# Macaron transformer block on one core: the light layers' token sum on VectorE stands ahead of its wait for the probabilities of the same pass

## The chip, the cores and the metric

One core of a Trainium2 chip runs the whole kernel as one launch. The metric is device time in microseconds (us), the median of several executions. One further execution was taken by the hardware profiler; all rows below are from it. Engines: TensorE (PE in the rows; PEld is its weight load), VectorE (DVE), ScalarE (ACT), GpSimd (POOL), SyncE (SP, the DMA queue).

## The reference, cut to what matters

8192 tokens (16 sequences of 512) of 128 channels go through six layers. Layers one and three are the same routed feed-forward layer with the same weights; each has a light part (attention in windows of 128 tokens, 8 heads of 64) and a heavy part on chosen tokens. What concerns the change is the light part and the sum onto the tokens:

```python
def light_local_attn(x, gamma, wq, wkv, wo):
    xn = rmsnorm(x, gamma)
    q = xn @ wq
    k, v = jnp.split(xn @ wkv, 2, axis=-1)
    # windows of 128 tokens, 8 heads
    attn = jax.nn.softmax(einsum('bwhid,bwhjd->bwhij', q * SCALE, k), axis=-1)
    out = einsum('bwhij,bwhjd->bwhid', attn, v)
    return out @ wo
...
x = x + 0.5 * _L0_ffn_ref(_layernorm(x), ...)   # layer 1 (f1)
x = x + _L0_attn_ref(_layernorm(x), ...)
x = x + 0.5 * _L0_ffn_ref(_layernorm(x), ...)   # layer 3 (f2)
```

Beside it the layer's router runs 50 iterations of a coordinate descent on 48 rows of 512 scores (`coor_descent`: a log-sum-exp, then a clamp), and then picks the top tokens.

## The kernel before, in words

`light_attention` runs twice, with tag `f1l` in layer one and `f2l` in layer three. There are 64 windows (`NT`), and they are software-pipelined: `windows` calls `body(i, ...)` on every engine for i = -1 to 66, and pass i works on several windows at once. Most passes are hardware loops unrolled by four (`Fori`), where addresses and semaphore values come out of registers; a few passes at the seams are written out. Each engine runs its own part of the pass strictly in the order written, and semaphores tie the engines together.

A pass on each engine, by line:

- TensorE: L400 the q and k projections of window i (`ps_qk`); L407 the output projection of window i-3 into `ps_a[:, 2]` (signals `f_ps`); L415 eight transposes of the probabilities of window i-2; L420 the v projection; L425 the transpose of the next window's normed tokens `xr` into `ps_a[:, 0]`, the same PSUM bank as L407's result, so that it waits for `y_ready`, the token sum of this same pass; L433 the scores of window i (`ps_s`); L449 probabilities times v (`ps_v`), which waits for ScalarE's copies of the turned probabilities and of v.
- ScalarE: L474 copies the attention output to `oT` (L407 of this pass reads it), L479 the exponential into `prob` (signals `p_sb`), L484 copies q and k, L465 and L467 exponential and logarithm of one descent step, L490 turned probabilities, L493 v, L496 the turned tokens `xrT`, then the second descent step.
- VectorE: L534 maximum of the scores, L538 subtracts it (`ssub`), L528, L522 and L523 settle one descent step and start the next (`na`, `nm`, `tmin`), L546 sums the probabilities (`rsum`, waits for `p_sb`), L550 reciprocal (`rec`), L554 the token sum `y = x + 0.5 * ps_a[:, 2]` (waits for `f_ps`; `g_y` in layer one, `g_x` in layer three), L513 makes `xr` of the window after next (it waits for L425, which reads the buffer before), then L528, L522 and L523 again for the second descent step.
- GpSimd: L371, two multiplications of half of the probabilities by `rec`, right after `rec_ready`.

The passes fall into stages. In passes 4 to 27 (24 passes, a hardware loop) the descent runs, two steps to a pass, and VectorE makes `xr`. In passes 28 to 59 ScalarE makes `xr` (L460) and VectorE instead picks eight maxima to a pass (L570, L573); of these, 32 to 59 (28 passes) are hardware loops.

Of the kernel before, what the change touches and what calls it, by code (L numbers as in the profile page):

```python
# [12 lines left out]
ALU = mybir.AluOpType  # L13
# [50 lines left out]
def past(i, n):  # L64

    return not isinstance(i, int) or i >= n
# [192 lines left out]
def light_attention(nc, tag, x, y, scale_a, shift_b, s_rows, smax, na, logk, posw, wparts, lw, hw, w, ident):  # L259
# [7 lines left out]
    with ExitStack() as ctx:  # L267
# [35 lines left out]
        ps_a = A.ps("ps_a", [P, 4, P])  # L303
# [3 lines left out]
        sum_ready, rec_ready, norm_ready, y_ready = (A.sem(n) for n in ("sum_ready", "rec_ready", "norm_ready", "y_ready"))  # L307
        xrT_ps, qk_ps, v_ps, s_ps, pT_ps, o_ps, f_ps = (
            A.sem(n) for n in ("xrT_ps", "qk_ps", "v_ps", "s_ps", "pT_ps", "o_ps", "f_ps"))
# [13 lines left out]
        def windows(eng, body, between):  # L323


            for i in range(-1, VB):
                body(i, i % VB, 0 if i == D0 else None, None)
            with eng.Fori(1, D1 // VB) as k:
                for u in range(VB):
                    body(VB * k + u, u, 2 * (VB * k) + 2 * (u - D0) - 1, None)  # L330
            for i in range(D1, D1 + VB):
                body(i, i % VB, None, i - D1)
            with eng.Fori(D1 // VB + 1, (D1 + RQ) // VB) as k:
                for u in range(VB):
                    body(VB * k + u, u, None, VB * k + u - D1)
            between(1)
            with eng.Fori((D1 + RQ) // VB, E0 // VB) as k:
                for u in range(VB):
                    body(VB * k + u, u, None, VB * k + u - D1)
            between(2)  # L340
            for i in range(E0, NT + 3):
                body(i, i % VB, None, None)

        def live(i, lag=0):
            return not isinstance(i, int) or 0 <= i - lag < NT

        def late(i, r):
            return r is not None or isinstance(i, int) and i >= D1

        def at(i, n):  # L350
            return isinstance(i, int) and i == n

        @block.sync
        def _(sp):
            sp.dma_start(hraw[:, 0:HID], w["wq_heavy"]).then_inc(hw_in, 16)
            sp.dma_start(hraw[:, HID:3 * HID], w["wkvT_heavy"]).then_inc(hw_in, 16)
            sp.dma_start(hgamma[:], w["gamma_heavy"].rearrange("(c o) -> c o", o=1)).then_inc(hw_in, 16)
            sp.dma_start(hw["wo"][:], w["wo_heavy"].rearrange("(p r) c -> r p c", r=P)).then_inc(hw_in, 16)
            sp.wait_ge(hw_in, 64)
# [148 lines left out]
        @block.vector  # L508
        def _(dve):
            ch = Chain(dve, step)  # L510

            def make_xr(j):
                nc.vector.scalar_tensor_tensor(xr[:], x[:, bass.ds(j, 1), :].rearrange("p o c -> p (o c)"), scale_a[:, bass.ds(j, 1)],  # L513
                                               shift_b[:, bass.ds(j, 1)].broadcast_to([P, C]), ALU.mult, ALU.add).then_inc(xr_ready, 1)

            make_xr(0)

            def descend(d):
                if past(d, 1):
                    dve.wait_ge(na_ready, d)  # L520
                    nc.vector.nop(nofuse=True)
                nc.vector.tensor_scalar(nm[:], smax[:], na[:], -1.0, ALU.min, ALU.mult)  # L522
                nc.vector.tensor_scalar(tmin[:], s_rows[:], na[:], None, ALU.min).then_inc(tmin_ready, 1)  # L523

            def settle(d):
                dve.wait_ge(lsum_ready, d + 1)
                nc.vector.nop(nofuse=True)
                nc.vector.tensor_scalar(na[:], lsum[:], nm[:], logk[:], ALU.subtract, ALU.subtract).then_inc(na_ready, 1)  # L528

            def body(i, u, d, r):  # L530
                if live(i, 1):
                    dve.wait_ge(s_ps, i)
                    sc = ps_s[:].rearrange("p s a b -> p (s a) b")
                    nc.vector.tensor_reduce(mx[:], sc, X_AX, ALU.max).then_inc(mx_ready, 1)  # L534
                    dve.wait_ge(mx_ready, i)
                    if past(i, 2):
                        dve.wait_ge(p_sb, i - 1)
                    nc.vector.tensor_tensor(ssub[:], sc, mx[:].rearrange("p (h o) -> p h o", o=1).broadcast_to([P, HEADS, P]),  # L538
                                            ALU.subtract).then_inc(sub_ready, 1)
                if d is not None:  # L540
                    if past(d, 1):
                        settle(d - 1)
                    descend(d)
                if live(i, 1):
                    dve.wait_ge(p_sb, i)
                    nc.vector.tensor_reduce(rsum[:], prob[(u - 1) % 2][:], X_AX, ALU.add).then_inc(sum_ready, 1)  # L546
                    dve.wait_ge(sum_ready, i)
                    if past(i, 3):
                        dve.wait_ge(norm_ready, 2 * i - 4)
                    nc.vector.reciprocal(rec[(u - 1) % 2][:], rsum[:]).then_inc(rec_ready, 1)  # L550
                if live(i, 3):
                    dve.wait_ge(f_ps, i - 2)
                    j = i - 3
                    nc.vector.scalar_tensor_tensor(  # L554
                        y[:, bass.ds(j, 1), :].rearrange("p o c -> p (o c)"), ps_a[:, 2], 0.5,
                        x[:, bass.ds(j, 1), :].rearrange("p o c -> p (o c)"), ALU.mult, ALU.add).then_inc(y_ready, 1)
                if live(i, -2) and not late(i, r):
                    dve.wait_ge(xrT_ps, i + 2)
                    make_xr(i + 2)
                if d is not None and past(d, 1):  # L560
                    settle(d)
                    descend(d + 1)
                if at(i, D1):
                    settle(ITERS - 2)
                    dve.wait_ge(na_ready, ITERS - 1)
                    nc.vector.tensor_scalar(tmin[:], s_rows[:], na[:], 0.0, ALU.subtract, ALU.min).then_inc(u_ready, 1)
                if r is not None:
                    dve.wait_ge(work_ready, r + 1)
                    nc.vector.nop(nofuse=True)
                    nc.vector.max(top[:], work[:]).then_inc(top_ready, 1)  # L570
                    dve.wait_ge(top_ready, r + 1)
                    nc.vector.nop(nofuse=True)
                    nc.vector.match_replace(work[:], top[:], work[:], -1.0).then_inc(work_ready, 1)  # L573
                if at(i, E0):
                    dve.wait_ge(filled, 1)
                    ch.step(nc.vector.tensor_tensor_scan(rank[:], ones[:], mask[:], 0.0, ALU.mult, ALU.add))
                if at(i, E0 + 1):
                    ch.step(nc.vector.tensor_tensor(rank[:], rank[:], mask[:], ALU.mult))
                    nc.vector.tensor_scalar(rank[:], rank[:], -1.0, None, ALU.add).then_inc(rank_ready, 1)
                if at(i, NT + 1):  # L580
                    dve.wait_ge(rows_ps, 1)
                    ch.step(nc.vector.tensor_copy(posw[:], ps_rows))
                    ch.step(nc.vector.tensor_copy(wparts[:, 0], posw[:, 1]))
                    ch.step(nc.vector.tensor_tensor(wrest[:], posw[:, 1], wparts[:, 0], ALU.subtract))
                    ch.step(nc.vector.tensor_copy(wparts[:, 1], wrest[:]))
                    ch.step(nc.vector.tensor_tensor(wparts[:, 2], wrest[:], wparts[:, 1], ALU.subtract))

            def between(n):
                if n == 1:
                    dve.wait_ge(work_ready, RQ + 1)  # L590
                    ch.step(nc.vector.tensor_scalar(mask[0:KV0, :], work[0:KV0, :], -1.0, None, ALU.is_equal))
                if n == 2:
                    dve.wait_ge(work_ready, RKV + 1)
                    ch.step(nc.vector.tensor_scalar(mask[KV0:ROWS, :], work[KV0:ROWS, :], -1.0, None, ALU.is_equal))

            windows(dve, body, between)


# [1826 lines left out]
```

## Time and profile before

| | |
|---|---|
| median of 3 executions | 3347.32 us (3339.31 to 3350.53) |
| the profiled execution | 3347.39 us |
| its span | 3345.6 us |
| granted TensorE clock, mean | 0.902 |
| TensorE busy | 2784.1 us (83%) |
| VectorE busy | 2343.1 us (70%) |
| ScalarE busy | 1850.5 us (55%) |
| GpSimd busy | 1479.8 us (44%) |

The span is the time between the first and the last instruction; the execution's own time has 1.8 us around it. The light part of layer one lies between about 54 and 534 us of the span, that of layer three between about 1592 and 2099 us.

### The profile page before, as it was taken

The numbers are of one execution on the slowest core, as the hardware profiler recorded it, in microseconds if no ns is written. First come the engines' busy times: TensorE is split into PE (matmuls) and PEld (weight loads), VectorE is DVE, ScalarE is ACT, GpSimd is POOL, SyncE is SP. The second block draws the span as 40 slices with busy tenths as digits, with TensorE's granted clock in tenths as the row PEclk, the third lists the DMA queues.
The fourth block names the chain that finished last, engine by engine and source line by source line (L and its number), as shares of the span: only waits on it lengthen the run. The fifth ranks groups of instructions, "written<-read, shape, count | busy, mean of one in ns | idle before, by whom it ended". The sixth has DMA issues, their size and how long they took to land. (4 is left out here: it accounts for less than half of the span.)

```text
span 3345.6 us, 72967 instructions
## 1 busy us (share of the span) xinstructions
PE 2784.1 (83%) x24552; PEld 1858.4 (56%) x24552; DVE 2343.1 (70%) x6126; ACT 1850.5 (55%) x3771; POOL 1479.8 (44%) x1662
## 2 busy tenths in 40 slices
PE   7999998996699999998888999899584278887674
PEld 4777886785233333333666777687452045555542
DVE  5887776885589888983777777688752267776741
ACT  3776664552167666664677666455431257775421
POOL 1222336772455555531222233776445254541445
PEclk9999999997599999999999999899785579999775
DMA  2000000001333333320000000000432355453532
GB/s 79 0 0 1 0 0 1 0 0 30 76 85 88 79 78 78 87 49 13 14 0 0 1 0 1 1 0 0 120 95 36 88 130 131 123 128 81 135 88 31
DMA packets 157597, 162.91 MB, mean 49 GB/s; under 512 B 43217, under 2 KB 136017, under 8 KB 157009
## 3 DMA queue, kind: packets, MB, share of 16 engines
q1 hardware_dynamic: 148176, 152.43, 17.6%
q0 software_dynamic: 9216, 7.87, 1.7%
q8 instruction: 114, 1.87, 0.2%
q14 instruction: 91, 0.74, 0.1%
HBM read 84.57 MB, written 74.60 MB: 48 GB/s over the span
## 5 line engine op out<-in xcount | busy, mean ns | idle before, releaser
L1700 DVE CUSTOM_DVE_ANT_0 la_ps<-la_ps,la_tri 128x512 f32<-128x512 f32 (+3 forms) x1024 | 481.0, 516 | 89.9 <-PE la_ps L1281 80.8
L1554 ACT ACTIVATE la_prob<-la_ps 128x512 f32<-128x512 f32 x640 | 373.8, 601 | 231.2 <-PE la_ps L1292 224.4
L371 POOL TENSOR_TENSOR f2l_prob<-f2l_prob,f2l_rec 128x512 f32<-128x512 f32 x128 | 132.4, 1056 | 361.2 <-DVE f2l_rec L550 361.2
L1281 PE MATMUL la_ps<-la_ks,la_qs 48*128 48x512 bf16 (+3 forms) x1024 | 255.1, 318 | 42.5 <-DVE la_mx L1700 26.8
L1181 POOL TENSOR_SCALAR_AFFINE_SELECT la_prob<-la_prob 128x512 f32<-128x512 f32 x256 | 160.0, 637 | 293.5 <-ACT la_prob L1554 293.3
L371 POOL TENSOR_TENSOR f1l_prob<-f1l_prob,f1l_rec 128x512 f32<-128x512 f32 x128 | 133.9, 1068 | 332.5 <-DVE f1l_rec L550 332.5
L1292 PE MATMUL la_ps<-la_qs,la_ks 50*128 50x512 bf16 (+3 forms) x1024 | 240.9, 308 | 5.1 <-ACT la_prob L1554 2.3
L1698 DVE TENSOR_REDUCE ca_mx<-ca_ps 128x4 f32<-128x512 f32 x256 | 162.7, 681 | 51.3 <-PE ca_ps L1281 51.1
L1324 PE MATMUL la_ps_o<-la_prob,la_v 128*32 128x512 f32 (+3 forms) x2048 | 195.7, 456 | 0.0
L1292 PEld LDWEIGHTS la_ps<-la_qs,la_ks 50*128 50x128 bf16 x1024 | 67.1, 94 | 231.2 <-ACT la_prob L1554 168.9
L1554 ACT ACTIVATE ca_prob<-ca_ps 128x512 f32<-128x512 f32 x256 | 140.3, 598 | 40.8 <-PE ca_ps L1292 38.9
L1700 DVE DVE_READ_ACCUMULATOR2_ANT la_mx<- 128x1 f32 x1024 | 144.8, 141 | 0.0
L400 PE MATMUL f2l_ps_qk<-f2l_xrT,f_wqkv 128*128 128x128 f32 x1024 | 133.0, 284 | 0.7 <-ACT f2l_xrT L496 0.7
L400 PE MATMUL f1l_ps_qk<-f1l_xrT,f_wqkv 128*128 128x128 f32 x1024 | 132.6, 283 | 0.7 <-ACT f1l_xrT L496 0.7
L1292 PE MATMUL ca_ps<-ca_qs,ca_ks 58*128 58x128 bf16 x1024 | 93.0, 226 | 45.1 <-DMA ca_ks<-stack_image 18.9
L1281 PEld LDWEIGHTS la_ps<-la_ks,la_qs 48*128 48x128 bf16 x1024 | 66.9, 95 | 111.7 <-DVE la_mx L1700 92.4
L400 PEld LDWEIGHTS f2l_ps_qk<-f2l_xrT,f_wqkv 128*128 128x128 f32 x1024 | 120.7, 194 | 11.7 <-issue 10.5
L400 PEld LDWEIGHTS f1l_ps_qk<-f1l_xrT,f_wqkv 128*128 128x128 f32 x1024 | 120.5, 193 | 11.7 <-issue 10.5
L1292 PEld LDWEIGHTS ca_ps<-ca_qs,ca_ks 58*128 58x128 bf16 x1024 | 62.0, 98 | 107.8 <-issue 65.6
L1166 POOL TENSOR_TENSOR ca_rr<-ca_qb,ca_t 128x512 f32<-128x512 f32 x32 | 43.7, 1366 | 169.2 <-ACT ca_t L1623 169.2
L546 DVE TENSOR_REDUCE f2l_rsum<-f2l_prob 128x8 f32<-128x1024 f32 x64 | 78.1, 1220 | 55.8 <-ACT f2l_prob L479 55.8
L546 DVE TENSOR_REDUCE f1l_rsum<-f1l_prob 128x8 f32<-128x1024 f32 x64 | 78.1, 1220 | 54.5 <-ACT f1l_prob L479 54.5
(552 smaller groups left out, 7990.5 us busy)
## 6 DMA issues: line engine op xcount, KB each, us to landing
stack_image<-la_parts SPq DMA_DIRECT2D x192, 128.0 KB, 2.4
stack_image<-ca_parts SPq DMA_DIRECT2D x192, 128.0 KB, 2.3
la_qs<-stack_image SPq DMA_DIRECT2D x64, 192.0 KB, 3.5
la_ks<-stack_image SPq DMA_DIRECT2D x64, 192.0 KB, 4.3
ca_qs<-stack_image SPq DMA_DIRECT2D x64, 192.0 KB, 3.9
ca_ks<-stack_image SPq DMA_DIRECT2D x64, 192.0 KB, 5.1
gather_table<-m_xn SPq DMA_DIRECT2D x32, 256.0 KB, 2.3
gather_table<-m_pr SPq DMA_DIRECT2D x32, 128.0 KB, 2.2
```

What stands on the lines that cost most here:

```text
L371: nc.gpsimd.tensor_tensor(pr[:, g], pr[:, g], rc[:, g].rearrange("p (h o) -> p h o", o=1).broadcast_to([P, PAIRS, P]), ALU.mult).then_inc( ...
L400: last = nc.tensor.matmul(ps_qk[:, t, p], wqkv[:, t, p * P:(p + 1) * P], xrT[:], start=True, stop=True)
L546: nc.vector.tensor_reduce(rsum[:], prob[(u - 1) % 2][:], X_AX, ALU.add).then_inc(sum_ready, 1)
L1166: nc.gpsimd.tensor_tensor(rr[:], left[:], right[:], op)
L1181: return nc.gpsimd.affine_select(view, view, pattern=[[0, 4], [1, P]], compare_op=ALU.is_ge, fill=0.0, base=0, channel_multiplier=-1)
L1281: last = nc.tensor.matmul(bank[:, col:col + width], qs[u][rows, h // 2, qblk * P:(qblk + 1) * P], ks[u][rows, h // 2, keys], start=True, s ...
L1292: last = nc.tensor.matmul(bank[:, col:col + width], ks[u][rows, h // 2, blk * P:(blk + 1) * P], qs[u][rows, h // 2, blk * P:blk * P + widt ...
L1324: last = nc.tensor.matmul(ps_o[32 * j:32 * j + 32, blk * P:T], v[u][:, blk, 4 * q + j, :], prob[q % 2][:, unit, col:col + width], start=bl ...
L1554: nc.scalar.activation(prob[q % 2][:, n], ps2[n % 2][:], ACT.Exp, scale=SM).then_inc(S["p_sb"], 1)
L1698: last = nc.vector.tensor_reduce(m, bank[:].rearrange("p (a b) -> p a b", a=TPB), X_AX, ALU.max)
L1700: last = nc.vector.tensor_tensor_reduce(bank[:, col:col + width], bank[:, col:col + width], tri[:, T - width:T], 1.0, -BIG, ALU.add, ALU.m ...
```

## The change

On VectorE the token sum (its wait for `f_ps` and the instruction) moves from behind the reciprocal to ahead of the wait for `p_sb`, in every pass that has one, in both light layers. No other engine's code is touched, and no wait is added or dropped.

```diff
                     descend(d)
+                if live(i, 3):
+                    dve.wait_ge(f_ps, i - 2)
+                    j = i - 3
+                    nc.vector.scalar_tensor_tensor(
+                        y[:, bass.ds(j, 1), :]..., ps_a[:, 2], 0.5,
+                        x[:, bass.ds(j, 1), :]..., ALU.mult, ALU.add).then_inc(y_ready, 1)
                 if live(i, 1):
                     dve.wait_ge(p_sb, i)
                     nc.vector.tensor_reduce(rsum[:], prob[(u - 1) % 2][:], X_AX, ALU.add).then_inc(sum_ready, 1)
...
                     nc.vector.reciprocal(rec[(u - 1) % 2][:], rsum[:]).then_inc(rec_ready, 1)
-                if live(i, 3):
-                    dve.wait_ge(f_ps, i - 2)
-                    j = i - 3
-                    nc.vector.scalar_tensor_tensor(
-                        y[:, bass.ds(j, 1), :]..., ps_a[:, 2], 0.5,
-                        x[:, bass.ds(j, 1), :]..., ALU.mult, ALU.add).then_inc(y_ready, 1)
                 if live(i, -2) and not late(i, r):
                     dve.wait_ge(xrT_ps, i + 2)
                     make_xr(i + 2)
```

Lines after it shift: in the changed kernel the token sum is L547, the sum of probabilities L552 and the reciprocal L556. On VectorE, a pass of layer three in the descent stage stood like this before, from the end of the first descent step to the making of `xr` (ISA and REGISTER_ALU rows are register instructions that the engine's sequencer does, for addresses and semaphore values):

```order
L523 TENSOR_SCALAR f2l_tmin<-f_s_rows,f_na 48x512
L545 ISA
L546 TENSOR_REDUCE f2l_rsum<-f2l_prob 128x8
L547 ISA
L549 ISA
L550 RECIPROCAL f2l_rec<-f2l_rsum 128x8
L552 ISA
L554 ISA x2
L554 SCALAR_TENSOR_TENSOR g_x<-f2l_ps_a,g_y 128x128
L558 ISA
L513 ISA x2
L513 REGISTER_ALU
```

And it stands like this in the changed kernel:

```order
L523 TENSOR_SCALAR f2l_tmin<-f_s_rows,f_na 48x512
L545 ISA
L547 ISA x2
L547 SCALAR_TENSOR_TENSOR g_x<-f2l_ps_a,g_y 128x128
L551 ISA
L552 TENSOR_REDUCE f2l_rsum<-f2l_prob 128x8
L553 ISA
L555 ISA
L556 RECIPROCAL f2l_rec<-f2l_rsum 128x8
L558 ISA
L513 ISA x2
L513 REGISTER_ALU
```

The token sum and its register instructions moved ahead of the sum of the probabilities; `xr` now follows the reciprocal directly. In layer one there are fewer register instructions; the same place of the descent stage, changed kernel:

```order
L523 TENSOR_SCALAR f1l_tmin<-f_s_rows,f_na 48x512
L547 ISA
L547 SCALAR_TENSOR_TENSOR g_y<-f1l_ps_a,g_x 128x128
L552 TENSOR_REDUCE f1l_rsum<-f1l_prob 128x8
L555 ISA
L556 RECIPROCAL f1l_rec<-f1l_rsum 128x8
L558 REGISTER_ALU
L513 ISA
L513 SCALAR_TENSOR_TENSOR f1l_xr<-g_x,g_a,g_b 128x128
```

One register instruction stands ahead of the token sum here and two in layer three; ahead of `xr` it is one here (the ISA row of L513) and three there. On the other engines the order of instructions is the same in both kernels.

## Rows read from the trace of the kernel before

**Rows 1.** Busy time by stretch, L479 alone (length, ACT busy, its count)

```profile
90.70:258.60 167.90, 23.27 (x22) 1.00 0.00 0
302.60:488.50 185.90, 27.48 (x26) 1.00 0.00 0
1629.90:1816.30 186.40, 23.31 (x22) 1.00 0.00 0
1861.30:2053.50 192.20, 27.48 (x26) 1.00 0.00 0
```

**Rows 2.** Waits in the first, third and fourth stretch (total us, times, longest)

```profile
PE f1l_ps_a L425 <- DVE g_y L554: 11.2, 22, 0.6
...
PE f2l_ps_a L425 <- DVE g_x L554: 25.1, 22, 1.2
...
PE f2l_ps_a L425 <- DVE g_x L554: 8.9, 26, 1.0
```

**Rows 3.** Timeline, one pass of layer one's descent stage (start, us, engine, line, idle before)

```profile
197.61 1.06 ACT L479 ACTIVATE f1l_prob<-f1l_ssub 128x1024 f32<-128x1024 f32 x1 [0.95 <-DVE f1l_ssub L538]
198.70 1.22 DVE L546 TENSOR_REDUCE f1l_rsum<-f1l_prob 128x8 f32<-128x1024 f32 x1 [0.33 <-ACT f1l_prob L479]
...
200.22 0.29 DVE L554 SCALAR_TENSOR_TENSOR g_y<-f1l_ps_a,g_x 128x128 f32 x1
200.34 2.09 POOL L371 TENSOR_TENSOR f1l_prob<-f1l_prob,f1l_rec 128x512 f32<-128x512 f32 x2 [5.51 <-DVE f1l_rec L550]
...
200.66 0.30 PE L425 MATMUL f1l_ps_a<-g_ident,f1l_xr 128*128 128x128 f32 x1 [0.46 <-DVE g_y L554]
201.14 0.38 DVE L513 SCALAR_TENSOR_TENSOR f1l_xr<-g_x,g_a,g_b 128x128 f32 x1 [0.63 <-PE f1l_ps_a L425]
201.36 0.59 ACT L493 COPY f1l_v<-f1l_ps_v 128x512 f32<-128x512 f32 x1
201.94 0.76 DVE L523 TENSOR_SCALAR f1l_tmin<-f_s_rows,f_na 48x512 f32<-48x512 f32 x1
...
205.01 1.06 PE L407 MATMUL f1l_ps_a<-f_wo,f1l_oT 128*128 128x128 f32 x8
205.29 1.06 ACT L479 ACTIVATE f1l_prob<-f1l_ssub 128x1024 f32<-128x1024 f32 x1 [0.74 <-DVE f1l_ssub L538]
```

**Rows 4.** Timeline, one pass of layer three's descent stage

```profile
1697.76 1.06 ACT L479 ACTIVATE f2l_prob<-f2l_ssub 128x1024 f32<-128x1024 f32 x1 [0.99 <-DVE f2l_ssub L538]
...
1700.53 2.04 POOL L371 TENSOR_TENSOR f2l_prob<-f2l_prob,f2l_rec 128x512 f32<-128x512 f32 x2 [6.43 <-DVE f2l_rec L550]
1700.98 0.33 PE L425 MATMUL f2l_ps_a<-g_ident,f2l_xr 128*128 128x128 f32 x1 [1.20 <-DVE g_x L554]
1701.80 0.92 DVE L513 SCALAR_TENSOR_TENSOR f2l_xr<-g_y,g_a,g_b 128x128 f32 x1 [0.87 <-PE f2l_ps_a L425]
...
1705.37 1.15 PE L407 MATMUL f2l_ps_a<-f_wo,f2l_oT 128*128 128x128 f32 x8
1706.24 1.06 ACT L479 ACTIVATE f2l_prob<-f2l_ssub 128x1024 f32<-128x1024 f32 x1 [1.00 <-DVE f2l_ssub L538]
```

**Rows 5.** Timeline, layer one's late stage, a pass where TensorE does not wait

```profile
431.85 1.06 PE L407 MATMUL f1l_ps_a<-f_wo,f1l_oT 128*128 128x128 f32 x8
434.69 0.30 PE L425 MATMUL f1l_ps_a<-g_ident,f1l_xr 128*128 128x128 f32 x1
438.92 1.06 PE L407 MATMUL f1l_ps_a<-f_wo,f1l_oT 128*128 128x128 f32 x8
```

**Rows 6.** Timeline, one pass of layer three's late stage

```profile
1987.35 1.06 PE L407 MATMUL f2l_ps_a<-f_wo,f2l_oT 128*128 128x128 f32 x8
1988.36 1.22 DVE L546 TENSOR_REDUCE f2l_rsum<-f2l_prob 128x8 f32<-128x1024 f32 x1 [1.24 <-ACT f2l_prob L479]
1990.17 0.59 ACT L493 COPY f2l_v<-f2l_ps_v 128x512 f32<-128x512 f32 x1
1994.64 1.06 ACT L479 ACTIVATE f2l_prob<-f2l_ssub 128x1024 f32<-128x1024 f32 x1 [1.04 <-DVE f2l_ssub L538]
```

More of the change, by code:

```diff
@@ L543, in body @@
                     descend(d)
+                if live(i, 3):
+                    dve.wait_ge(f_ps, i - 2)
+                    j = i - 3
+                    nc.vector.scalar_tensor_tensor(
+                        y[:, bass.ds(j, 1), :].rearrange("p o c -> p (o c)"), ps_a[:, 2], 0.5,
+                        x[:, bass.ds(j, 1), :].rearrange("p o c -> p (o c)"), ALU.mult, ALU.add).then_inc(y_ready, 1)
                 if live(i, 1):
@@ L550, in body @@
                     nc.vector.reciprocal(rec[(u - 1) % 2][:], rsum[:]).then_inc(rec_ready, 1)
-                if live(i, 3):
-                    dve.wait_ge(f_ps, i - 2)
-                    j = i - 3
-                    nc.vector.scalar_tensor_tensor(
-                        y[:, bass.ds(j, 1), :].rearrange("p o c -> p (o c)"), ps_a[:, 2], 0.5,
-                        x[:, bass.ds(j, 1), :].rearrange("p o c -> p (o c)"), ALU.mult, ALU.add).then_inc(y_ready, 1)
                 if live(i, -2) and not late(i, r):
```

## Prediction, made before the changed kernel was timed

> **What bounds the kernel now.** I read first how long a pass takes. The exponential (L479) runs once a pass, so the length of a stretch over its count is the pass time [rows 1]: 167.90 / 22 = 7.63 us in layer one's descent stage, 185.90 / 26 = 7.15 in its late stage, 186.40 / 22 = 8.47 and 192.20 / 26 = 7.39 in the same stages of layer three. The second column of times there says nothing more, but the clock (the 1.00 behind the count) does: TensorE ran at its full level throughout, so no stage is slow for that.
>
> Then I read who waits for the token sum. TensorE's L425 does, in every pass: 11.2 us over 22 passes of layer one's descent stage (0.51 a pass), 25.1 over 22 in layer three (1.14), 8.9 over 26 in its late stage (0.34) [rows 2]. All of that wait goes away in the best case. Whether a pass gets shorter by it is the question, so I followed one pass in each timeline.
>
> Layer one, descent [rows 3]. Exponential at 197.61, sum of probabilities at 198.70 (1.09 later), GpSimd's pair at 200.34 (1.64 later) until 202.43, the end of `tmin` at 201.94 + 0.76 = 202.70, which is 0.27 behind GpSimd's end, and the next exponential at 205.29 (2.59 later). 1.09 + 1.64 + 2.09 + 0.27 + 2.59 = 7.68, the whole pass. The reader is to see that the token sum (200.22) and L425 are not in this chain: `tmin` is held until GpSimd has finished both halves. `xr` starts at 201.14, 0.18 behind the end of L425, and ends at 201.52, 0.13 behind the middle of the pair (200.34 + 1.04 = 201.38): it is held too, but by the first half alone.
>
> The Trainium skill (SBUF — State Buffer, section Who interferes with whom) says that VectorE shares a port pair with GpSimd, taken for a whole instruction by whoever starts first, and that VectorE wants it for two SBUF inputs while GpSimd reads SBUF (`xr`), and in the fast modes of `tensor_scalar` (`tmin`). The trace agrees with it. It is the rule that speaks against the change: without it, in the sum for layer three's descent stage below, `xr` would end at 3.66 + 0.38 = 4.04 and `tmin` at 4.04 + 0.42 + 0.76 = 5.22 at the latest instead of 5.72, which would make 0.25 a pass or 6 us more of gain.
>
> Layer three, descent [rows 4]. L425 starts at 1700.98, `xr` only 0.82 behind it (three register instructions stand ahead of it), at 1701.80, when the second half (from 1701.55) is under way. So it ends at 1702.72, 0.15 behind the pair's end at 1702.57, and the next exponential comes 3.52 later, at 1706.24. Here the token sum's place does cost: later L425, later `xr`, the wrong half.
>
> Late stages. TensorE alone needs 438.92 - 431.85 = 7.07 a pass where it does not wait [rows 5]. Layer one is at 7.15, nearly there; layer three is 0.32 above.
>
> **The change part by part.** Nothing is added or removed; one instruction of 0.29 and its wait move. Two things follow. L425 no longer waits for the sum: it can start 434.69 - 431.85 = 2.84 behind L407 [rows 5]. And VectorE now waits for L407's result ahead of the sum of probabilities, so behind that wait stand `rsum`, `rec`, `xr` and the second descent step, and GpSimd, which waits for `rec`.
>
> How long is it from L407's end to the token sum? No row has it in a loop. The nearest are `xr` behind L425: 0.18 with one register instruction ahead [rows 3], 1701.80 - 1701.31 = 0.49 with three [rows 4]. The sum has one in layer one and two in layer three: I take 0.18 and 0.35, with 0.18 and 0.49 as ends. So, counted from L407's start, `rsum` can start at 1.06 + 0.18 + 0.29 + 0.02 = 1.55 in layer one, and 1.06 + 0.35 + 0.29 + 0.03 = 1.73 in layer three. The 0.02 or 0.03 is the gap that an instruction behind another has.
>
> When is L407? In a descent pass it comes from ScalarE: v's copy ends at 201.95, 4.34 behind the exponential, L407 of the next pass starts 3.06 after that, at 205.01 [rows 3], so 7.40 behind the exponential, and the token sum is not in this either. With pass time P, two chains then close over two passes: exponential, 7.40, L407, then `rsum`, then the next exponential.
>
> - Layer one, descent: from `rsum` to the next exponential it is 7.63 - 1.09 = 6.54, through GpSimd. 2P = 7.40 + 1.55 + 6.54 = 15.49, P = 7.75, **0.12 longer**. Times 24 passes: +2.9 us. Can `xr` do better? L425 could start at 2.84, `xr` at 2.84 + 0.48 = 3.32 behind L407, GpSimd's pair at 1.55 + 1.64 = 3.19. It misses by 0.13, and is held by the first half as before. The moved wait costs, and nothing is gained.
> - Layer three, descent: GpSimd starts 1.68 behind `rsum` (1700.53 against 1697.76 + 1.09), so at 3.41 behind L407; its first half lasts until 4.43. `xr` is due at 2.84 + 0.82 = 3.66, inside the first half, not the second. It ends near 4.57, `tmin` is then due at 4.57 + 0.42 = 4.99 (the 0.42 as between 201.52 and 201.94 [rows 3]), inside the second half, and ends 0.27 behind it at 5.72; the next exponential at 5.72 + 2.6 = 8.32, 6.59 behind `rsum`. L407 is 7.61 behind the exponential now [rows 4], where ScalarE's second descent step was late too; with that earlier I take 7.50 (ends 7.40 and 7.61). 2P = 7.50 + 1.73 + 6.59 = 15.82, P = 7.91, **0.56 shorter**. Times 24: -13.4 us.
> - Layer three, late: from `rsum` to the next exponential 1994.64 - 1988.36 = 6.28 [rows 6], less the token sum's 0.29: 5.99. With 1.73 the exponential is 7.72 behind L407, so 0.65 behind the next L407 instead of just ahead of it. Does ScalarE then hold TensorE? v's copy ends at 1990.76, 3.49 behind the exponential (1988.36 - 1.09 = 1987.27), and 3.06 more make 6.55. 2P = 7.72 + 6.55 = 14.27, P = 7.13, just above TensorE's 7.07. 7.39 - 7.13 = 0.26, times 28: -7.3 us.
> - Layer one, late: between 7.15 and 7.07; I take 7.12, times 28: -0.8 us (ends 0 and -2.2).
> - The written-out passes: 12 of each layer; I take nothing for them (ends 0 and -2). What hides the later `rec` in the late stages is that the transposes of these probabilities (L415) stand in the next pass, behind its L407: GpSimd ends at 1.73 + 1.68 + 2.04 = 5.45 behind L407 and the next L407 starts at 7.07 at the earliest, so 1.6 us are left; with that cover gone L415 would be late next.
>
> Sum: 2.9 - 13.4 - 7.3 - 0.8 = -18.6. From the profiled execution's own 3347.39 (the median is 3347.32, the same): **3329 us**. The unknown gap moves it little: 0.14 either way is 0.07 a pass over 24 + 24 + 28 passes, 5 us; 7.40 or 7.61 for 7.50 moves it 1 us.
>
> **The rivals.**
>
> - *`xr` gets ahead of GpSimd.* The misses above are 0.13 us in layer one and 0.25 in layer three, as small as the gaps that I took from neighbours: a longer way to the token sum delays GpSimd but not L425. Then `tmin` is due within the first half and ends a half pair earlier, 1.04 or 1.02 off 2P. Layer one: 14.45 / 2 = 7.23, -9.6 for +2.9; layer three: 14.80 / 2 = 7.40, -25.7 for -13.4. One of them gives about 3316, both 3304. Against it: both sums say that it misses. The skill's page has whoever starts first win, so that GpSimd would then wait for `xr`, 0.35 us that these figures leave out. Chance 0.24, mostly for one.
> - *Layer three's descent doesn't profit.* `xr` is still due in the second half, because its register instructions, not L425, make it late. For it: the 0.82. Against it: it would have to be 4.43 - 3.66 = 0.77 later. 8.47 stays: 3329 + 13 = 3342. Chance 0.11.
> - *The moved wait holds VectorE (slower).* VectorE stands at `f_ps` while the probabilities are ready; `rec`, GpSimd, `tmin` and the exponential all come later. Each 1 us of extra gap is 0.5 a pass in both descent stages and the late one of layer three: 38 us (24 + 14). The gain is gone at 0.49 more than I took, and at 0.75 more the time is 3357. For it: layer one's +2.9 is this. Against it: the largest such gap in the rows is 0.49 in all. Chance 0.05.
>
> **How the numbers follow.** As forecast 0.60, its own range 3321 to 3335 by the ends above. The first rival 0.24, the second 0.11, the third 0.05. The range goes to 3311 below (one layer of the first rival with its ends) and 3342 above, which leaves the third rival and the case of both layers outside. A change of 0.3% (10 us, to 3337) is about what a measurement of this kernel can tell from none. Faster: forecast and first rival but for a little, 0.81; same: the second rival and a rest of the forecast, 0.13; slower 0.06.
>
> **What the changed kernel's profile would show.** The wait of L425 for the token sum is gone in all stages, and VectorE's idle time ahead of L547 is named after L407. Pass times 7.75, 7.12, 7.91 and 7.13. In layer three `xr` ends just behind the middle of GpSimd's pair and the second `tmin` of a pass behind its end; in layer one both stay as they are. If a descent pass is near 7.3, `xr` has got ahead of GpSimd; if layer three's `xr` still ends behind the pair, the second rival holds; if `rsum` starts more than 2 us behind L407, the gap was larger than I took.

## The result, and the profile after

The changed kernel takes 3303.31 us (median of 4 executions, 3298.66 to 3315.69), against 3343.55 us for the kernel before in the same comparison: ratio 0.9884, with a 95% interval of 0.9855 to 0.9913. That is faster by about 40 us. The forecast was faster, but by 18.6, and 3303 lies below the range of 3311 to 3342. (The forecast started from 3347.39; this comparison's median for the same kernel is 3.8 lower, which is spread between executions.) The profiled execution is the slowest of the four: 3315.69 us, span 3313.9.

The stretches that answer to [rows 1], in the changed kernel (length, then ScalarE's busy time and the count of exponentials):

```profile
91.70:260.70 169.00, 23.28 (x22) 1.00 0.00 0
304.20:483.10 178.90, 27.51 (x26) 1.00 0.00 0
1627.10:1798.30 171.20, 23.31 (x22) 1.00 0.00 0
1841.90:2020.70 178.80, 27.52 (x26) 1.00 0.00 0
```

Length over count gives the pass time. All pass times of this document are read so, but where it says from one L407 to the next:

| us a pass | before | forecast | changed | over all passes of the stage |
|---|---|---|---|---|
| layer one, descent | 7.63 | 7.75 | 7.68 | +1.2 (24 passes) |
| layer one, late | 7.15 | 7.12 | 6.88 | -7.6 (28) |
| layer three, descent | 8.47 | 7.91 | 7.78 | -16.6 (24) |
| layer three, late | 7.39 | 7.13 | 6.88 | -14.3 (28) |

The last column adds up to -37.3. One row says the same for each layer as a whole, the exponentials of both light parts, in the kernel before and in the changed one (the last two times are the starts of the first and the last exponential):

```profile
L479 ACT ACTIVATE f1l_prob<-f1l_ssub x64: 1056/1057/1064, 64.1 to 523.5; 128x1024 f32<-128x1024 f32 x64
L479 ACT ACTIVATE f2l_prob<-f2l_ssub x64: 1056/1057/1063, 1602.5 to 2088.5; 128x1024 f32<-128x1024 f32 x64
```

```profile
L479 ACT ACTIVATE f1l_prob<-f1l_ssub x64: 1056/1058/1063, 64.8 to 517.6; 128x1024 f32<-128x1024 f32 x64
L479 ACT ACTIVATE f2l_prob<-f2l_ssub x64: 1056/1058/1064, 1599.3 to 2055.0; 128x1024 f32<-128x1024 f32 x64
```

459.4 + 486.0 = 945.4 us before, 452.8 + 455.7 = 908.5 after: 36.9 less. The rest of the two spans differs the other way by 5.2 (3345.6 - 945.4 = 2400.2 against 3313.9 - 908.5 = 2405.4), in layers that the change does not touch. What the change does is therefore read from the light layers below; 3 to 4 of the 40 us are not resolved.

The waits in layer three's late stage of the changed kernel, which answer to the third line of [rows 2]:

```profile
DVE g_x L547 <- PE f2l_ps_a L407: 26.4, 25, 1.1
ACT f2l_oT L474 <- PE f2l_ps_v L449: 18.9, 26, 0.8
PEld f2l_ps_s L433 <- issue: 13.5, 26, 1.3
PEld f2l_ps_a L425 <- issue: 6.2, 26, 0.2
```

L425 no longer waits for the token sum; VectorE instead waits for L407, about 1.06 a pass, as forecast. One pass of that stage in its timeline, to be held against [rows 5, 6]:

```profile
1999.87 1.06 PE L407 MATMUL f2l_ps_a<-f_wo,f2l_oT 128*128 128x128 f32 x8
...
2000.29 1.06 ACT L479 ACTIVATE f2l_prob<-f2l_ssub 128x1024 f32<-128x1024 f32 x1 [1.52 <-DVE f2l_ssub L538]
...
2001.23 0.29 DVE L547 SCALAR_TENSOR_TENSOR g_x<-f2l_ps_a,g_y 128x128 f32 x1 [1.07 <-PE f2l_ps_a L407]
...
2001.44 1.21 DVE L552 TENSOR_REDUCE f2l_rsum<-f2l_prob 128x8 f32<-128x1024 f32 x1
...
2002.50 0.27 PE L425 MATMUL f2l_ps_a<-g_ident,f2l_xr 128*128 128x128 f32 x1
...
2003.10 0.61 ACT L493 COPY f2l_v<-f2l_ps_v 128x512 f32<-128x512 f32 x1
...
2006.71 1.06 PE L407 MATMUL f2l_ps_a<-f_wo,f2l_oT 128*128 128x128 f32 x8
...
2007.14 1.06 ACT L479 ACTIVATE f2l_prob<-f2l_ssub 128x1024 f32<-128x1024 f32 x1 [1.54 <-DVE f2l_ssub L538]
```

L425 stands 2.63 behind L407, not 2.84, and TensorE's pass, from one L407 to the next, is 6.84, not 7.07 (6.88 over the whole stretch, which has one longer pass). The forecast took both larger numbers for TensorE without a wait. The 6.84 is no single case: from one L407 to the next it is 6.83 or 6.84 in 24 of 26 passes of layer one's late stage and in 23 of layer three's.

One pass of layer three's descent stage, to be held against [rows 4]:

```profile
1696.75 1.06 PE L407 MATMUL f2l_ps_a<-f_wo,f2l_oT 128*128 128x128 f32 x8
1697.17 1.06 ACT L479 ACTIVATE f2l_prob<-f2l_ssub 128x1024 f32<-128x1024 f32 x1 [1.00 <-DVE f2l_ssub L538]
...
1698.33 1.21 DVE L552 TENSOR_REDUCE f2l_rsum<-f2l_prob 128x8 f32<-128x1024 f32 x1
...
1699.98 2.09 POOL L371 TENSOR_TENSOR f2l_prob<-f2l_prob,f2l_rec 128x512 f32<-128x512 f32 x2 [5.72 <-DVE f2l_rec L556]
1700.19 0.99 DVE L513 SCALAR_TENSOR_TENSOR f2l_xr<-g_y,g_a,g_b 128x128 f32 x1 [0.28 <-issue]
...
1701.59 0.76 DVE L523 TENSOR_SCALAR f2l_tmin<-f_s_rows,f_na 48x512 f32<-48x512 f32 x1
...
1704.98 1.06 ACT L479 ACTIVATE f2l_prob<-f2l_ssub 128x1024 f32<-128x1024 f32 x1 [1.00 <-DVE f2l_ssub L538]
```

`xr` starts in GpSimd's first half and ends at 1701.18, 0.16 behind that half's end (1699.98 + 1.04 = 1701.02); `tmin` ends at 1702.35, 0.28 behind the pair's end.

### The profile page after: what moved, and what is told of

Same layout as the page of the kernel before. It is cut to its first block and busy times, and to the rows that moved or that the text cites. A ratio compares the mean times of both kernels' runs of the same rounds, so it can differ in the third digit from the quotient of the medians.

```text
span 3313.9 us, 72967 instructions
## 1 busy us (share of the span) xinstructions
PE 2770.5 (84%) x24552; PEld 1868.3 (56%) x24552; DVE 2356.1 (71%) x6126; ACT 1840.0 (56%) x3771; POOL 1478.4 (45%) x1662
## 5 line engine op out<-in xcount | busy, mean ns | idle before, releaser
L479 ACT ACTIVATE f2l_prob<-f2l_ssub 128x1024 f32<-128x1024 f32 x64 | 67.8, 1059 | 85.7 <-DVE f2l_ssub L538 83.0
L479 ACT ACTIVATE f1l_prob<-f1l_ssub 128x1024 f32<-128x1024 f32 x64 | 67.7, 1058 | 79.4 <-DVE f1l_ssub L538 79.4
```

The costliest lines, as they stand in the source:

```text
L479: nc.scalar.activation(prob[(u - 1) % 2][:], ssub[:], ACT.Exp, scale=SM).then_inc(p_sb, 1)
```

## The experiments

The theory after the result: in the late stages TensorE's own pass is 6.83, and the row from which I had 7.07 hid a wait for the token sum; in the descent stages GpSimd's pair of multiplications holds `xr` and `tmin`, so that the token sum's place counts there mainly by the half in which `xr` falls. The rival explanations are named with the runs. Edits are against the kernel before unless said otherwise.

**The late passes alone.**

```diff
+                if live(i, 3) and late(i, r):
+                    ... token sum ...
                 if live(i, 1):
                     dve.wait_ge(p_sb, i)
...
-                if live(i, 3):
+                if live(i, 3) and not late(i, r):
                     ... token sum ...
```

> The token sum is moved only in the passes without a descent step (28 and later). Read by pass time (length of a stretch over its exponentials). My theory now: in the late stage TensorE alone needs 6.83 a pass, and the 7.07 that I took for it still held a wait of L425 for the token sum; so the late stages come out at 6.83 to 6.85 in both layers and the descent stages stay at 7.63 and 8.47: about 8 and 15 us less in the two layers, 3320 in all. Rival: the late stage gains only because it enters with another phase from the changed descent stage; then it stays at 7.15 and 7.39 here and the time at 3343.

Measured: 3320.0 us (ratio 0.9916, 0.9894 to 0.9938). Its stretches, descent and late of each layer:

```profile
91.40:259.30 167.90, 23.28 (x22) 1.00 0.00 0
302.70:481.60 178.90, 27.50 (x26) 1.00 0.00 0
1624.10:1810.40 186.30, 23.31 (x22) 1.00 0.00 0
1856.40:2035.20 178.80, 27.52 (x26) 1.00 0.00 0
```

7.63 and 8.47 in the descent, 6.88 in both late stages over the whole stretch. (The 6.83 to 6.85 is the pass time without the one longer pass of the stretch, where VectorE makes a mask between two loops.) The late gain stands without the descent stage's; the rival of a carried phase falls. TensorE's L407 to L407 is 6.83 or 6.84 here too, in all but 2 and 3 passes of the two stages.

**The descent passes alone.** The same edit with the two conditions exchanged.

> The token sum is moved only in the passes with the descent (up to 27). My theory: layer one's descent stage 7.68 a pass (0.05 more than before), layer three's 7.78 (0.69 less), late stages as before at 7.15 and 7.39: 1 us more and 17 less, 3328 in all. Rival: layer three's descent gained from elsewhere, then it stays at 8.47. With the run of the late stage alone, the two gains should add up to that of the change within 3 us of light layers' time.

Measured: 3336.15 us (ratio 0.9966, 0.9951 to 0.998). Stretches: 169.10 / 22 = 7.69, 185.90 / 26 = 7.15, 171.20 / 22 = 7.78, 192.20 / 26 = 7.39. Both stages do here what they do in the changed kernel and nothing else. First to last exponential, the late passes alone save 21.3 us (451.3 and 472.8), the descent passes alone 14.0 (461.0 and 470.4); together 35.3, against 36.9 of the change. The time of the descent passes alone is 8 above the 3328 that I expected: the light layers saved 2 less, and the whole 10 us against the kernel before, which is 4 less than the light layers alone. Differences of a few us between whole times are not explained here.

**The token sum between the sum of probabilities and the reciprocal.** It keeps its place behind the probabilities; only the reciprocal is no longer ahead of it.

```diff
                     nc.vector.tensor_reduce(rsum[:], prob[(u - 1) % 2][:], X_AX, ALU.add).then_inc(sum_ready, 1)
+                if live(i, 3):
+                    dve.wait_ge(f_ps, i - 2)
+                    ... token sum ...
+                if live(i, 1):
                     dve.wait_ge(sum_ready, i)
                     ... reciprocal ...
-                if live(i, 3):
-                    dve.wait_ge(f_ps, i - 2)
-                    ... token sum ...
```

> The token sum stands between the sum of probabilities and the reciprocal: no wait for L407 ahead of the sum of probabilities, and L425 is released some 0.2 (layer one) to 0.4 us (layer three) earlier than before. My theory (L425 releases TensorE, and decides for xr in layer three): late stages 6.9 and 7.1, layer three's descent 8.0, layer one's descent 7.8 since the reciprocal and GpSimd are some 0.2 later; 22 us less than before in all, 3321. Rival (what counts is that VectorE uses its idle time ahead of the probabilities): no gain, since the instruction stays in the busy part: 7.1 to 7.4 late, 3343.

Measured: 3306.73 us (ratio 0.9874, 0.9851 to 0.9896), better than expected and as good as the change. Pass times 7.62, 6.87, 7.75 and 6.88. The timeline of one of its passes in layer three's descent shows what I had missed:

```profile
1703.04 1.22 DVE L546 TENSOR_REDUCE f2l_rsum<-f2l_prob 128x8 f32<-128x1024 f32 x1 [0.35 <-ACT f2l_prob L479]
1704.18 0.28 DVE L550 SCALAR_TENSOR_TENSOR g_x<-f2l_ps_a,g_y 128x128 f32 x1
1704.43 0.20 DVE L557 RECIPROCAL f2l_rec<-f2l_rsum 128x8 f32<-128x8 f32 x1
...
1704.72 2.09 POOL L371 TENSOR_TENSOR f2l_prob<-f2l_prob,f2l_rec 128x512 f32<-128x512 f32 x2 [5.68 <-DVE f2l_rec L557]
1705.23 0.67 DVE L513 SCALAR_TENSOR_TENSOR f2l_xr<-g_y,g_a,g_b 128x128 f32 x1 [0.60 <-PE f2l_ps_a L425]
```

The reciprocal starts 1.39 behind the start of the sum that it reads, with the token sum in between. In the pass of [rows 4], kernel before, it is the same without one:

```profile
1698.86 1.22 DVE L546 TENSOR_REDUCE f2l_rsum<-f2l_prob 128x8 f32<-128x1024 f32 x1 [0.36 <-ACT f2l_prob L479]
1700.25 0.20 DVE L550 RECIPROCAL f2l_rec<-f2l_rsum 128x8 f32<-128x8 f32 x1 [0.17 <-DVE f2l_rsum L546]
```

The reciprocal waits for `sum_ready` in both. So the token sum costs VectorE nothing in that gap, and the reciprocal is not later; my 0.2 was wrong. The rival falls too: the instruction stays behind the probabilities, and the late stages are as short as with the change. These runs also answer whether 6.84 hides a wait in its turn, for ScalarE's copies. L449 starts 0.1 us behind the end of v's copy (L493) in layer three's late stage of the changed kernel, 0.3 in layer one's and 0.5 in both here, and L407 to L407 is 6.83 or 6.84 in all of them. A releaser that can come 0.4 us earlier without a shorter pass is not what TensorE waits for. `xr` falls into GpSimd's first half and ends at 1705.90, 0.14 behind the half's end (1704.72 + 1.04 = 1705.76).

**The reciprocal behind the second descent step, on top of the change.**

```diff
                     ... sum of probabilities ...
+                if live(i, 1) and not (d is not None and past(d, 1)):
                     dve.wait_ge(sum_ready, i)
                     ... reciprocal ...
...
                 if d is not None and past(d, 1):
                     settle(d)
                     descend(d + 1)
+                if live(i, 1) and (d is not None and past(d, 1)):
+                    dve.wait_ge(sum_ready, i)
+                    if past(i, 3):
+                        dve.wait_ge(norm_ready, 2 * i - 4)
+                    nc.vector.reciprocal(rec[(u - 1) % 2][:], rsum[:]).then_inc(rec_ready, 1)
```

Passes without two descent steps keep the reciprocal at its place.

> On top of the change, in the descent passes the reciprocal (and with it GpSimd's pair) stands behind the second descent step instead of ahead of xr. My theory: the second tmin, held until GpSimd's pair ends, sets the descent pass; with GpSimd starting only behind it, the descent stages fall from 7.68 and 7.78 to 7.2 to 7.4, some 10 us less in each layer than with the change, 3283 in all. Rival: something else holds the pass at 7.7 (ScalarE's v copy and TensorE), then nothing changes, or the later reciprocal makes the transposes late and a pass is longer than 7.8.

Measured: 3287.79 us (ratio 0.9833, 0.9806 to 0.986). The descent passes fall to 158.80 / 22 = 7.22 and 161.30 / 22 = 7.33 (means: a pass of 6.7 and one of 7.8 to 8.0 take turns). From its timeline in layer three:

```profile
1692.29 0.35 DVE L513 SCALAR_TENSOR_TENSOR f2l_xr<-g_y,g_a,g_b 128x128 f32 x1 [0.54 <-PE f2l_ps_a L425]
...
1693.05 0.47 DVE L523 TENSOR_SCALAR f2l_tmin<-f_s_rows,f_na 48x512 f32<-48x512 f32 x1
1693.44 0.18 DVE L568 RECIPROCAL f2l_rec<-f2l_rsum 128x8 f32<-128x8 f32 x1
...
1693.71 2.04 POOL L371 TENSOR_TENSOR f2l_prob<-f2l_prob,f2l_rec 128x512 f32<-128x512 f32 x2 [5.75 <-DVE f2l_rec L568]
```

`xr` takes 0.35 and `tmin` 0.47 where no multiplication runs beside them; 0.92 and 0.38 was `xr`, 0.76 `tmin` in [rows 3, 4]. GpSimd's work moved behind them and ends at 1695.75; the waits of the stage have no TensorE wait for GpSimd, so its result still comes in time. The rival (something else holds the pass at 7.7) is refuted.

**GpSimd's multiplications shortened, with the token sum at its old place and at its new one.** In the passes up to 27 each of the two instructions multiplies one head instead of four; the kernel leaves out the rest of the normalisation there.

```diff
+                    width = PAIRS if late(i, r) else 1
                     for n in range(2):
-                        g = slice(PAIRS * n, PAIRS * n + PAIRS)
+                        g = slice(PAIRS * n, PAIRS * n + width)
```

> The kernel before, but in the passes up to 27 GpSimd multiplies one head of four in each of its two instructions (the other heads' probabilities stay unnormalised, so this part of the computation is left out): the pair lasts about 0.6 us instead of 2.04. My theory (the pair holds xr and tmin, and in layer one hides the place of the token sum): the second tmin then follows xr without being held; from L425 3.05 behind the exponential I get 7.3 a pass in layer one (7.63 before) and, from 3.2, 7.9 in layer three (8.47). Rival (xr and tmin are long for another reason): xr and tmin keep their 0.92 and 0.76 us, and the pass times stay.

> The changed kernel with the same shortened multiplications up to pass 27 (three heads of four stay unnormalised). My theory: without GpSimd's hold the token sum's place counts in layer one's descent stage too: 7.2 and 7.3 a pass, that is 0.1 and 0.6 below the same kernel with the sum at its old place; xr about 0.35 us and tmin 0.47. Rival (the moved wait for L407 is what lengthened layer one's descent by 0.05, with or without GpSimd): 7.3 or more in layer one, no better than with the old place.

Measured, one profile each (3326.11 and 3291.3 us), old place then new place, the descent stretch of layers one and three:

```profile
91.70:253.00 161.30, 23.31 (x22) 1.00 0.00 0
...
1625.10:1797.60 172.50, 23.35 (x22) 1.00 0.00 0
```

```profile
91.00:249.90 158.90, 23.29 (x22) 1.00 0.00 0
...
1614.20:1775.70 161.50, 23.28 (x22) 1.00 0.00 0
```

7.33 and 7.84 with the old place, 7.22 and 7.34 with the new. So with GpSimd's hold gone the new place is worth 0.11 a pass in layer one, where with the hold it costs 0.05; in layer three 0.50. The pass times of the new place are those of the late reciprocal within 0.01, by a different edit to the same hold. The shortened pair lasts 0.80 us (twice 0.40), not the 0.6 that I expected. In the run with the old place, each `xr` and `tmin` is short, so the rival (long for another reason) falls:

```profile
L514 DVE SCALAR_TENSOR_TENSOR f2l_xr<-g_y,g_a,g_b x30: 302/352/354, 1588.0 to 1801.5; 128x128 f32 x24, 128x128 f32<-128x128 f32 x6
...
L524 DVE TENSOR_SCALAR f2l_tmin<-f_s_rows,f_na x49: 468/470/473, 1609.9 to 1802.3; 48x512 f32<-48x512 f32 x49
```

With the new place `tmin` takes 0.47 too, but `xr` is not free everywhere: 0.52 to 0.53 in layer one's descent, beside the shortened multiplication, where I had expected 0.35.

**The changed kernel again.**

> The changed kernel once more, to tell what of its 40 us lies in the light layers. My theory: first to last exponential 452.8 and 455.8 us again (before 459.4 and 486.0), 37 us less, and all else within the run-to-run spread; 3300 to 3310 in all. Rival: some of the gain lies in other layers, then a stretch outside the light layers is shorter than before by more than 2 us again.

Measured: 3307.74 us, the kernel before 3348.72 in the same comparison (ratio 0.9897, 0.9851 to 0.9942). The exponentials of the light layers run 453.5 and 455.2 us (before: 459.4 and 486.0). Stretches outside: from the last exponential of layer one to the first of layer three 1079.9 us (before 1079.0, changed 1081.7); behind layer three's last 1248.9, where the kernel before had 1257.1 and the changed kernel in its first profile 1258.9. That last stretch moved by 10 us between two profiles of the same kernel, so single spans can't tell a few us. By its letter the rival's sign is there in this run (8.2 us shorter than before), but the first profile had the same stretch 1.8 longer, so it is no gain that repeats; a gain of a few us outside the light layers is neither shown nor excluded. Inside them, readings from one profile do repeat: the four stretches take 169.00, 178.90, 171.20 and 178.80 us again, to the tenth.

**The late reciprocal without the change.** The edit of the late reciprocal on the kernel before, where the token sum then directly follows the sum of probabilities in the descent passes.

> The kernel before with only the reciprocal moved behind the second descent step in the descent passes; the token sum then follows the sum of probabilities directly there and is where it was in the late stage. My theory: GpSimd's hold is gone and the token sum fills the gap behind the sum of probabilities, so the descent passes come out as short as with both moves, 7.2 to 7.4, with the late stages at 7.12 and 7.37: 8 and 27 us less, 3311 in all. Rival (the wait for L407 must stand ahead of the probabilities for the descent to reach 7.2 to 7.3): 7.5 or more in the descent stages.

Measured: 3309.62 us (ratio 0.9869, 0.9833 to 0.9905). Descent 159.10 / 22 = 7.23 and 161.60 / 22 = 7.35, late 186.00 / 26 = 7.15 and 192.30 / 26 = 7.40. The wait for L407 need not stand ahead of the probabilities for that, and the rival falls; the late stages, where nothing moved, stay at the times of the kernel before.

**A filler behind the token sum.** On the changed kernel:

```diff
                         x[:, bass.ds(j, 1), :]..., ALU.mult, ALU.add).then_inc(y_ready, 1)
+                    nc.vector.tensor_reduce(idle[:], x[:, 0:4, :], X_AX, ALU.max)
```

> The changed kernel with one more VectorE instruction (a maximum over 128x512 values into a tile that nobody reads, about 0.66 us) between the token sum and the sum of probabilities, in every pass that has a token sum. It prices the rival that the moved wait holds VectorE: all that stands behind the wait comes 0.66 later, the release of L425 doesn't. My theory (two passes close through L407, token sum, sum of probabilities, next exponential, v's copy, L407; in the changed kernel 1.56 + 5.73 + 6.42 = 13.71, 6.85 a pass in layer three's late stage, beside TensorE's own 6.83): half of it a pass, 7.1 to 7.2 in both late stages and about 8.0 to 8.1 in the descent stages. Rival (TensorE alone sets the late stage, VectorE has slack there): 6.83 to 6.86 stay in the late stages.

Measured, one profile (3370.27 us; span 3368.6, of which 2425.3 lie outside the light layers' exponentials, 20 more than in the changed kernel's first profile, in layers that the filler does not touch): 176.10 / 22 = 8.00, 184.00 / 26 = 7.08, 179.00 / 22 = 8.14, 185.80 / 26 = 7.15. The filler takes 0.67; the descent passes grow by 0.32 and 0.36, half of it, the late ones by 0.20 and 0.27, less than half. In the late stages one pass of two still takes about 6.84 to 6.9 from L407 to L407, and the other 7.2 in layer one and 7.3 to 7.4 in layer three. So the chain over two passes is real, and in the changed kernel it lies a little under TensorE's own pass: by 0.34 - 0.20 = 0.14 a pass in layer one and 0.34 - 0.27 = 0.07 in layer three (estimates, the half of the filler less the growth). TensorE sets the late stages there. The rival (VectorE has slack) holds for these 0.07 to 0.14 and no more.

**Token sum in the gap, reciprocal late.** The edit of the run between sum and reciprocal and that of the late reciprocal together, without the move ahead of the probabilities.

> The token sum right behind the sum of probabilities in every pass (as in the run with it between sum and reciprocal), and the reciprocal behind the second descent step in the descent passes. My theory: late stages 6.83, descent stages 7.23 and 7.35, so the same as the changed kernel with the late reciprocal: 58 us less than before, 3288. Rival (the two moves stand in each other's way, since the token sum no longer has the gap ahead of the reciprocal in the descent passes): 7.5 or more in the descent.

Measured: 3283.5 us (ratio 0.9811, 0.9784 to 0.9838). 159.10 / 22 = 7.23, 178.70 / 26 = 6.87, 161.60 / 22 = 7.35, 178.80 / 26 = 6.88. It has the lowest median here, 63 us under the kernel before, and within its interval the same as the late reciprocal on top of the change.

## Why the prediction was wrong

The direction and the mechanisms of the descent stages held: L425 lost its wait, VectorE took one for L407, layer one's descent did not gain, layer three's did because `xr` fell into GpSimd's first half. The size did not: -18.6 forecast, -37 in the light layers. Of the 18.7 between them, 6.8 and 7.0 lie in the two late stages, 3.2 and 1.7 in the descent stages of layers three and one.

**The step that failed** is in the late stages: "TensorE alone needs 438.92 - 431.85 = 7.07 a pass where it does not wait". It did wait in that pass. The rows of the kernel before that stand beside [rows 5] are these:

```profile
433.62 1.02 PE L420 MATMUL f1l_ps_v<-f_wqkv,f1l_xrT 128*128 128x512 f32 x2
434.25 0.29 DVE L554 SCALAR_TENSOR_TENSOR g_y<-f1l_ps_a,g_x 128x128 f32 x1
...
434.65 0.14 PEld L425 LDWEIGHTS f1l_ps_a<-g_ident,f1l_xr 128*128 128x128 f32 x1 [0.84 <-issue]
```

The token sum ends at 434.54, and L425 starts at 434.69, 0.15 behind it, as where the wait is named (200.51 and 200.66 in [rows 3]). The distance is 0.14 or 0.15 in all 26 passes of this stage, although the matmul carries the mark in 7 of them only, and in the 22 marked passes of layer one's descent (in layer three it is 0.05 or 0.06, in every pass). The row of the matmul shows no idle time, because the matmul ahead of it, L420, is drawn until 434.64; the idle time is on the weight load, 0.84 put down to "issue". I read the missing mark as no wait. The waits of the late stages before, which [rows 2] has not or only for the matmul, say it as totals (layer one, then layer three):

```profile
PEld f1l_ps_a L425 <- issue: 24.0, 26, 1.8
...
PE f1l_ps_a L425 <- DVE g_y L554: 2.4, 7, 1.0
```

```profile
PEld f2l_ps_a L425 <- DVE g_x L554: 30.4, 26, 1.8
...
PE f2l_ps_a L425 <- DVE g_x L554: 8.9, 26, 1.0
```

In the changed kernel the weight load's idle time is 6.2 in both. (Not all of it was lost before: part of it lies beside L420.) TensorE's pass without the wait is 6.84, and 2.84 from L407 to L425 is 2.63; the late passes alone, with the descent as it was, show the same. So layer one's late stage was not at 0.08 above its floor but at 0.3: -0.8 us forecast, -7.6 measured. In layer three no chain, however short, could have brought the sum under 7.07, that is -9.0, where -14.3 was measured. The 7.07 alone thus accounts for some 12 of the 18.7 (6.8 and 5.3).

In **layer three's late stage** (-7.3 forecast, -14.3 measured) the chain over two passes is there, but each of its three terms was too long: L407 to `rsum` 1.57 for 1.73 (the token sum comes 1.36 behind L407, and `rsum` starts 0.21 behind the token sum's start, before its end), `rsum` to the next exponential 5.70 for 5.99, exponential to the next L407 6.42 for 6.55. 13.69 / 2 = 6.85 for 7.13. The 5.99 left in two things that went with the token sum: 0.16 of idle time ahead of it, and a wait of about 0.16 of the maximum of the scores (L534) for TensorE's L433, which ended at 1991.87 in the pass of [rows 6], 0.05 ahead of it. That 6.85 equals TensorE's 6.84 proves nothing by itself, since such terms of a repeating pass add up to two passes whatever holds it; it is the filler that puts this chain some 0.07 a pass under TensorE.

**Layer three's descent** (-13.4 and -16.6): 7.91 forecast, 7.78 measured. In the pass shown above, exponential to L407 is 1704.51 - 1697.17 = 7.34 for 7.50, L407 to `rsum` 1698.33 - 1696.75 = 1.58 for 1.73, `rsum` to the next exponential 6.65 for 6.59: 15.57 / 2 = 7.78. `xr` is held by the first half and `tmin` by the second, as forecast. **Layer one's descent** (+2.9 and +1.2): the sign was right. The chain was too long here too: L407 to `rsum` is 1.43 for 1.55 (229.86 and 231.29), and the sum of probabilities is 0.05 to 0.17 late in about half of the passes only. A change of 0.05 a pass is small, but it came out in all three profiles with the whole pair of multiplications and the token sum ahead of the probabilities (169.0, 169.1 and 169.0 us, for 167.9 in the kernel before and with the late passes alone). This row pair of the changed kernel shows `xr` starting with GpSimd and held all the same:

```profile
209.81 1.22 DVE L513 SCALAR_TENSOR_TENSOR f1l_xr<-g_x,g_a,g_b 128x128 f32 x1
...
209.83 2.08 POOL L371 TENSOR_TENSOR f1l_prob<-f1l_prob,f1l_rec 128x512 f32<-128x512 f32 x2 [5.59 <-DVE f1l_rec L556]
```

**The rivals.** `xr` ahead of GpSimd was given 3304 for both layers, and 3303 was measured: the number is right by luck, since `xr` is held by GpSimd's first half in both layers (in a few passes of layer one it starts 0.02 ahead, as above, and gains nothing) and the descent passes are near 7.7, not 7.2 to 7.4. Being rid of the hold is worth what I had said, though: the late reciprocal does it, by another way, and gives 7.22 and 7.33 (7.23 and 7.40 in the sum). That layer three's descent doesn't profit: refuted, 7.78. The moved wait holds VectorE: not here, but its price in the descent was right, 0.32 to 0.36 a pass for a filler of 0.67; in the late stages it is less, for TensorE hides a part.

The range was too narrow below for the same reason as the sum: as end for layer one's late stage I had let the 7.07 stand, so no case of mine had more than 2.2 us there, and in layer three's that floor allowed 9.0 at most. Even the 37.3 of the table would have ended at 3310, just outside. (One reading is off by a hundredth: `xr` in [rows 3] ends 0.14, not 0.13, behind the middle of the pair; nothing hangs on it.)

## What to carry to other kernels

A floor of an engine read off a row without a wait mark needs a second look: hold the start of the instruction against the end of whoever could release it, and look at the weight load's idle time as well as the matmul's. A constant distance behind the same releaser in marked and unmarked passes (0.14 or 0.15 us here, in 7 and 19 passes) means that it waits in all of them.

The terms of a chain that closes over a repeating pass always add up to the pass, so their sum alone doesn't show that the chain sets it. A filler in the chain does: it costs its full share where the chain sets the pass (0.32 to 0.36 of 0.67 / 2 in the descent), and less where something else does.

When an instruction must leave a critical place, the gap between a reduction and the reciprocal that reads it may take it at no cost; it need not go ahead of a wait. And when VectorE instructions are long beside GpSimd's, ask whether GpSimd's work can be started later instead of sooner: here it began 1.4 to 2.7 us later in the descent passes, and TensorE, which reads its result, still never waited for it.

## What of the hardware was not expected

- A 128x128 `scalar_tensor_tensor` that by its row started 0.02 us ahead of GpSimd's first multiplication still took 1.22 us and ended 0.16 behind that multiplication's end (209.83 + 1.04 = 210.87), instead of the 0.35 that it takes alone. By the Trainium skill (SBUF — State Buffer, section Who interferes with whom) the first to issue wins; the recorded starts, 0.02 apart, do not settle which did.
- VectorE's reciprocal starts 1.33 to 1.40 us behind the start of the 1.22 us reduction that it reads and whose semaphore it waits for (1.39 in both passes shown; a little less, 1.24 to 1.26, in passes written out), with or without a 0.28 us instruction between them.
- Between GpSimd's two multiplications one held VectorE instruction gets through: in the changed kernel `xr` ends 0.14 to 0.16 behind the first, `tmin` 0.27 to 0.29 behind the second. The pair takes 2.09 us then, and 2.04 where no `xr` stands beside its first half.
